# Adding expert rows straight onto the output by accumulating indirect DMAs, in place of a scattered copy that is reloaded and combined

## Chip, cores and metric

One core of a Trainium2 chip runs the whole program. The metric is the device time of one execution in microseconds (us), the median over runs.

## The reference, cut to what matters

A transformer block on 2 sequences of 1024 tokens of width 128, all in float32. The first half (convolution, linear attention, a dense mixture of 4 experts) gives a residual stream `x` after its own scaling by `ga`. The second half, which the change touches, is a routed mixture of 8 experts in which each token uses two of them, and each expert has room for 512 rows:

```python
    h = _layernorm(x, axis=-1) * (1 + cb) + sb
    x = x + gb * _L0_ffn_ref(h, L0_ffn_wg, L0_ffn_w_gate, L0_ffn_w_down)
    # inside _L0_ffn_ref, tokens = h as 2048 rows, C = 512:
    h = jax.nn.gelu(jnp.einsum('ecd,edf->ecf', disp, w_gate), approximate=False)
    eo = jnp.einsum('ecf,efd->ecd', h, w_down).reshape(Ee * C, Dd)
    out = (g1 * keep1)[:, None].astype(x.dtype) * eo[f1] + (g2 * keep2)[:, None].astype(x.dtype) * eo[f2]
```

So each token's output row is its residual row plus `gb` (one row of 128 numbers for each of the two sequences) times the sum of at most two weighted expert rows. An expert slot that holds no token gives nothing.

## The kernel before

Tokens are 16 tiles of 128 rows, worked in 4 blocks of 4 tiles (BT = 4). The first half runs as a software pipeline of 23 steps whose order is written out by hand on each engine, with a semaphore for every hand-over. There is no scheduler: each engine and each queue runs its list in order, and a wait holds all that stands behind it.

The residual after the first half (`x_sb`, "x3" in the names of the semaphores) is made block by block, for blocks 0 to 2 on GpSimd (POOL, lines 387 to 391) and for the last on VectorE (DVE, lines 934 to 940). After that each token's normalised row is written with its number and its two weights (rows of 131 numbers) into the DRAM tensors `line1` and `line2`, a place per expert, by 32 indirect DMAs on POOL's queue (`scatters`, L417). SyncE (SP) waits for the counts (L311), appends the second choices to the first ones (`append`, L307), and loads each expert's 512 rows into SBUF (`rows(e)`, L323, `phi<-line` in the trace).

Then come the 8 experts of 512 rows each, e = 0 to 7. For each:

- TensorE (PE) transposes the rows (L1465), makes the up products (three passes over split operands, in four PSUM banks) and the down products of the expert before. The order on PE is: transposes of e+2, up of e+1, down of e (lines 1485 to 1492); up and down of the last expert close it (lines 1493 to 1497).
- ScalarE (ACT) copies the transposed rows with rounding (L708) and runs four GELUs of 128x512 (L270).
- DVE works out row numbers (`row_addresses`, L1069 to L1076), the low part of the split (L1158), and evacuates the four down products of 128x128, scaled by the row's weight, into the staging buffers `xh` (even experts) or `xm` (odd ones) (L1177).
- POOL issues four indirect DMAs of 128 rows, one per tile (L460), that write the rows into the DRAM tensor `chosen`: 2048 rows for first choices, 2048 for second choices, and behind these a place for empty slots. Rows of `chosen` that no expert writes must be zero, so SP zeroes its first 4096 rows early on (L299).

The last stage waits until all 32 of these DMAs have landed (L328), reloads both halves of `chosen` by 8 DMAs of 256 KB (L331), adds them on POOL (L466), multiplies by `gb` (`modb[..., 3, :]`, L1183) and adds the residual (L1185) on DVE, and stores the output by four DMAs of 256 KB (L334), block by block:

```python
            for half in chosen_written:
                sp.wait_ge(half, 16 * BT * E2 // 2)
            for b in range(NBLK):
                for k in range(2):
                    sp.dma_start(tiles(back[:, k], b), tiles(cv[:, k], b)).then_inc(back_in[b], 16)
            for b in range(NBLK):
                sp.wait_ge(comb_ready, b + 1)
                sp.dma_start(tiles(ov, b), tiles(x_sb, b)).then_inc(stored, 16)
```

DVE's evacuation of expert e from e = 2 on waits until the DMAs of expert e-2 have landed, since the staging buffer is the same.

Of the kernel before, what the change touches and what calls it, by code (L numbers as in the profile page):

```python
# [63 lines left out]
N_CONST = C_TRASH + E2 * BT  # L64


def block_kernel(nc, x, small, proj, wmod, w1, w2, b2, w_up, w_down, const, cmask, out):
    with ExitStack() as ctx:
# [8 lines left out]

        chosen = nc.dram_tensor("chosen", (2 * TOKENS + SLOTS, D), F32).ap()

# [83 lines left out]
        trash = sb("trash", [P, E2, BT])  # L163
        addr = sb("addr", [P, 4, BT])
        row_w = sb("row_w", [P, E2, BT])
        back_i = sb("back_i", [P, E2, BT], U32)

        back = wide[:, 0:TILES * 2 * D].rearrange("p (k t d) -> p k t d", t=TILES, k=2)
# [41 lines left out]
        chosen_written = [sem(f"chosen_written_{i}") for i in range(2)]  # L210
        back_in = L("back_in")
        both_ready, comb_ready, stored = sem("both_ready"), sem("comb_ready"), sem("stored")
# [46 lines left out]
        def xstage(e):  # L259
            return (xh if e % 2 == 0 else xm)[:]  # L260
# [15 lines left out]
        def _(sp):  # L276
            xv = x.rearrange("b (t p) d -> p (b t) d", p=P)
            ov = out.rearrange("b (t p) d -> p (b t) d", p=P)
# [18 lines left out]
            cz = chosen[0:2 * TOKENS, :].rearrange("(p r) d -> p (r d)", p=P)  # L297
            for i in range(BT):
                sp.dma_start(cz[:, i * 1024:(i + 1) * 1024], zero).then_inc(zeroed, 16)  # L299
# [6 lines left out]
            def append(e):  # L306
                sp.dma_start(line1[bass.ds(first[e] + e * LINE1, CAP), :],  # L307
                             line2[e * LINE2:e * LINE2 + CAP, :]).then_inc(moved[e], 16)

# [16 lines left out]
            cv = chosen[0:2 * TOKENS, :].rearrange("(k t p) d -> p k t d", k=2, p=P)  # L326
            for half in chosen_written:
                sp.wait_ge(half, 16 * BT * E2 // 2)  # L328
            for b in range(NBLK):
                for k in range(2):  # L330
                    sp.dma_start(tiles(back[:, k], b), tiles(cv[:, k], b)).then_inc(back_in[b], 16)  # L331
            for b in range(NBLK):
                sp.wait_ge(comb_ready, b + 1)
                sp.dma_start(tiles(ov, b), tiles(x_sb, b)).then_inc(stored, 16)  # L334
            sp.wait_ge(stored, 16 * NBLK)
# [3 lines left out]
        def _(pool):  # L339
# [115 lines left out]
            for e in range(E1):  # L455
                split(2 * E1 + e)
            for e in range(E2):
                for j in range(BT):
                    pool.wait_ge(eout_ready, BT * e + j + 1)
                    g.indirect_dma_start(out=chosen, out_offset=bass.IndirectOffsetOnAxis(back_i[:, e, j:j + 1], 0),  # L460
                                         in_=xstage(e)[:, j, :], in_offset=None).then_inc(chosen_written[e % 2], 16)

            for blk in range(NBLK):
                pool.wait_ge(back_in[blk], 32)
                a, b_ = tiles(back[:, 0], blk), tiles(back[:, 1], blk)
                g.tensor_tensor(a, a, b_, ALU.add).then_inc(both_ready, 1)  # L466
# [3 lines left out]
        def _(act):  # L470
# [20 lines left out]
            def high_part(k):  # L491

                act.wait_ge(wst_in[k // E1], 16)
                if k == E1:
                    act.wait_ge(zeroed, 16 * (E2 + BT))
# [207 lines left out]

            for e in range(E2):
# [4 lines left out]
                if e >= 1:  # L709
                    gelus(act, e - 1)  # L710
            gelus(act, E2 - 1)

        @block.vector
        def _(dve):
# [219 lines left out]
            def residual3(blk):  # L934
# [4 lines left out]
                step(v.tensor_tensor(tiles(x_sb, blk), acc[:], tiles(x_sb, blk), ALU.add))  # L939
                after()  # L940
# [115 lines left out]
            def slot_kinds():  # L1056
# [4 lines left out]
                step(v.scalar_tensor_tensor(trash[:], second[:], -float(TOKENS),  # L1061
                                            c_sb[:, C_TRASH:].rearrange("p (e t) -> p e t", e=E2), ALU.mult, ALU.add))
                after()
# [486 lines left out]
```

## Time and profile before

| | |
|---|---|
| median of 3 runs | 376.99 us (375.58 to 377.82) |
| profiled execution, span from first to last instruction | 385.2 us |
| own time of the profiled execution outside the span | none is given; the span is its time here |
| busy: PE, DVE, POOL, ACT | 72%, 60%, 42%, 38% of the span |
| the 8 experts, from the first transposed rows to the last evacuation | 299.8 to 363.7 us |
| from the last landing in `chosen` to the end | 368.2 to 385.2 us |
| TensorE's granted clock, mean over the span | 0.877 |

The profile is of one execution, on one core, with the profiler on; it is 8.2 us longer than the median of the runs shown. Times in the rows are us from the span's start. A row of the timeline gives start, duration, engine, line, operation, output and inputs, and in brackets the idle time of the engine before it and what ended that. The chain is the work that ended last, followed back step by step.

### The profile page before, as it was taken

The page shows a single profiled execution, that of the slowest core. Times are in us where ns is not written, and L with a number is a line of the kernel's source. Part 1 is how long each engine was busy: PE and PEld are TensorE (multiplying, and loading weights), DVE is VectorE, ACT ScalarE, POOL GpSimd, SP SyncE. Part 2 cuts the span into 40 slices and gives each one's busy share as a digit, 9 for nine tenths or more (in the row PEclk, how much of TensorE's full clock was granted, in tenths as well). Part 3 has the DMA queues.
Part 4 walks back from the last instruction along what each step waited for, and adds up shares of the span by engine and source line. Part 5 has one row for each costly group of instructions (what it writes and reads, how often), then busy time and mean ns, then how long its engine had stood idle before and what let it go on. Part 6 is the DMA issues. An engine that isn't in the chain of part 4 may idle for free.

```text
span 385.2 us, 4892 instructions
## 1 busy us (share of the span) xinstructions
PE 276.5 (72%) x1586; PEld 216.5 (56%) x1586; DVE 230.0 (60%) x678; ACT 148.2 (38%) x278; POOL 161.6 (42%) x165
## 2 busy tenths in 40 slices
PE   2736677656999998988999879994303799999300
PEld 2313333343867687576887768883202589998300
DVE  2478999969578876787498516757550332432116
ACT  3750452358443654326435634450110454451000
POOL 3235585292722126315022532152748116466533
PEclk9995969978699999999999989998555599999955
DMA  7993003000300000000000010000113634211165
GB/s 225 411 375 124 1 1 111 0 1 0 111 1 2 0 2 1 0 3 0 2 0 3 21 37 0 3 29 28 35 37 105 181 101 124 64 41 43 41 195 145
DMA packets 18312, 25.01 MB, mean 65 GB/s; under 512 B 2032, under 2 KB 14448, under 8 KB 17520
## 3 DMA queue, kind: packets, MB, share of 16 engines
q1 hardware_dynamic: 16240, 20.46, 16.4%
q0 software_dynamic: 2048, 4.25, 3.3%
q8 instruction: 13, 0.21, 0.2%
q14 instruction: 11, 0.09, 0.1%
HBM read 15.16 MB, written 11.68 MB: 70 GB/s over the span
## 4 chain that ended last, share of the span: by engine, by line
PE 30%; DVE 12%; issue 6%; DMA 4%; POOL 3%; another core or an unknown queue 3%; ACT 2%; SPq 1%; ACTq 0%; POOLq 0%; DVEq 0%
PE ps L1201 28%; POOL line L417 2%; DVE acc L929 2%; DMA wide<-chosen 1%; DMA phi<-line 1%; PE ps L1465 1%; DVE x_sb L1185 1%; DVE wide L1183 1%; PE ps L1222 1%; DVE nd L852 1%; DMA line<-h3r,dest_i 1%; DVE st L736 1%; ACT hid L600 1%; DVE qp L840 1%
## 5 line engine op out<-in xcount | busy, mean ns | idle before, releaser
L1201 PE MATMUL ps<-w_sb,hid 128*128 128x128 f32 x512 | 63.3, 283 | 5.2 <-DVE acc L929 3.4
L1201 PEld LDWEIGHTS ps<-w_sb,hid 128*128 128x128 f32 x512 | 61.4, 199 | 7.3 <-DVE acc L929 4.0
L600 ACT ACTIVATE hid<-ps,s_sb 128x512 f32<-128x512 f32 x64 | 43.0, 685 | 32.7 <-PE ps L1201 24.9
L414 POOL TENSOR_TENSOR kv<-phi,vx 128x1152 f32<-128x1152 f32 x16 | 38.0, 2375 | 35.0 <-DVE phi L831 15.7
L1201 PE MATMUL ps<-kv,c_sb 128*128 128x512 f32 (+1 forms) x96 | 41.2, 541 | 3.9 <-DVE qp L840 2.0
L417 POOL DMA_INDIRECT line<-h3r,dest_i x32 | 31.4, 980 | 23.3 <-DVE dest_i L1047 14.6
L1201 PE MATMUL ps<-h2h,w1h 128*128 128x512 f32 x80 | 37.1, 463 | 0.5 <-ACT hid L600 0.3
L1201 PE MATMUL ps<-h2l,w1h 128*128 128x512 f32 x80 | 32.5, 407 | 0.0
L1201 PE MATMUL ps<-h2h,w1l 128*128 128x512 f32 x80 | 32.5, 406 | 0.0
L840 DVE TENSOR_TENSOR qp<-ps,phi 128x1024 f32<-128x1024 f32 x16 | 19.5, 1221 | 21.3 <-PE ps L1201 11.6
L1201 PE MATMUL ps<-wd_sb,hid 128*128 128x128 f32 x256 | 30.2, 276 | 1.2 <-issue 1.2
L1201 PEld LDWEIGHTS ps<-wd_sb,hid 128*128 128x128 f32 x256 | 29.8, 192 | 2.2 <-issue 1.6
L929 DVE SCALAR_TENSOR_TENSOR acc<-ps,gwp,acc 128x128 f32<-128x128 f32 x64 | 18.0, 344 | 16.8 <-remote 8.9
L1201 PEld LDWEIGHTS ps<-kv,c_sb 128*128 128x128 f32 x96 | 18.0, 208 | 16.5 <-issue 13.7
L361 POOL TENSOR_SCALAR ve<-mv 128x4 f32<-128x4 f32 x12 | 3.3, 273 | 55.4 <-DVE mv L739 55.3
L460 POOL DMA_INDIRECT chosen<-xh,back_i x16 | 15.4, 961 | 23.7 <-DVE xh L1177 19.7
L270 ACT ACTIVATE hid<-ps 128x512 f32<-128x512 f32 x32 | 19.2, 599 | 12.3 <-PE ps L1201 9.8
L852 DVE TENSOR_REDUCE nd<-qp 128x144 f32<-128x1152 f32 x16 | 21.5, 1345 | 0.1
L460 POOL DMA_INDIRECT chosen<-xm,back_i x16 | 15.3, 959 | 12.3 <-DVE xm L1177 9.0
L708 ACT ACTIVATE h2h<-ps 128x512 fp32r<-128x512 f32 x8 | 4.8, 598 | 39.5 <-PE ps L1465 39.5
L1201 PEld LDWEIGHTS ps<-h2h,w1h 128*128 128x128 f32 x80 | 15.6, 195 | 5.6 <-issue 3.3
L1201 PEld LDWEIGHTS ps<-h2h,w1l 128*128 128x128 f32 x80 | 15.6, 195 | 3.8
(199 smaller groups left out, 535.8 us busy)
## 6 DMA issues: line engine op xcount, KB each, us to landing
line<-wuh SPq DMA_DIRECT2D x8, 262.0 KB, 13.2
line<-line SPq DMA_DIRECT2D x8, 262.0 KB, 3.0
phi<-line SPq DMA_DIRECT2D x8, 262.0 KB, 3.2
wd_sb<-in_w_down SPq DMA_DIRECT2D x1, 2048.0 KB, 12.3
chosen<-wuh SPq DMA_DIRECT2D x4, 512.0 KB, 11.5
wst<-in_w_up SPq DMA_DIRECT2D x2, 1024.0 KB, 5.0
wide<-chosen SPq DMA_DIRECT2D x8, 256.0 KB, 4.9
x_sb<-in_x SPq DMA_DIRECT2D x4, 256.0 KB, 7.3
```

The source lines that it names most:

```text
L270: nc.scalar.activation(hid[:, e % 2, c, :], ps[:, 2 + c, :], ACT.Gelu).then_inc(ehid_ready, 1)
L414: g.tensor_tensor(o_, k_, v_, ALU.mult).then_inc(kv_ready, 1)
L417: g.indirect_dma_start(out=(line1, line2)[k], out_offset=bass.IndirectOffsetOnAxis(dest_i[:, t, k:k + 1], 0), in_=h3r[:, t, :], in_offset= ...
L460: g.indirect_dma_start(out=chosen, out_offset=bass.IndirectOffsetOnAxis(back_i[:, e, j:j + 1], 0), in_=xstage(e)[:, j, :], in_offset=None) ...
L600: a_.activation(hid[:, e % 2, u % FC, :], ps[:, B_UP[u % 2], :], ACT.Silu, bias=s_sb[:, c:c + 1]).then_inc(hid_ready, 1)
L708: a_.activation(h2h[:, e % 2, :], ps[:, e % 2, :], ACT.Copy).then_inc(rowsT_hi, 1)
L736: step(v.bn_stats(st[:, j, :], src[:, j, :]))
L840: v.tensor_tensor(qp[:, 0:DH * D].rearrange("p (m c) -> p m c", m=DH), ps[:, B_KV:B_KV + 2, :].rearrange("p b (m c) -> p (b m) c", m=4), q ...
L852: a = step(v.tensor_reduce(nd[:, 0, :], qp[:].rearrange("p (c d) -> p c d", d=DH), AX.X, ALU.add))
L929: last = v.scalar_tensor_tensor(acc[:, j, :], ps[:, mix_bank(e), j * D:(j + 1) * D], gwp[:, e // E1 % 2, c:c + 1], acc[:, j, :], ALU.mult, ...
L1183: step(v.tensor_tensor(a, a, modb[:, blk // BPB, 3, None, :].broadcast_to([P, BT, D]), ALU.mult))
L1201: return m.matmul(o, l, r, start=start, stop=stop)
```

## The change

The output tensor gets 512 spare rows (SPARE) behind its 2048, which take the empty slots. SP stores the residual `x_sb` into the output as soon as each block of it is there, and zeroes the spare rows. The 8x4 indirect DMAs of POOL now go to the output and add to it (`compute_op=ALU.add`). The factor `gb` must therefore be in the rows before: `gate_rows` makes, for each tile of each expert, the row of `gb` that belongs to the token's sequence, from the masks `half` (token number at most 1024, or above), by an ACT product (`gsel`) and a DVE multiply-add, and the evacuation multiplies by it. Two experts may add to the same row, so POOL waits before the first DMA of expert e until those of expert e-1 have landed (semaphores `added`), and before the first of all until the residual is stored. `chosen`, its zeroing, its reload, the sum, the product, the residual add and the stores at the end are gone.

```diff
 C_ID, C_TRI, C_BD, C_COS, C_SIN, C_REV, C_TOK, C_SLOT, C_TRASH = 0, 128, 256, 400, 464, 528, 536, 552, 556
-N_CONST = C_TRASH + E2 * BT
+N_CONST = C_TRASH + BT
+SPARE = BT * P
...
-        chosen = nc.dram_tensor("chosen", (2 * TOKENS + SLOTS, D), F32).ap()
...
         second = sb("second", [P, E2, BT])
-        trash = sb("trash", [P, E2, BT])
         addr = sb("addr", [P, 4, BT])
+        half = sb("half", [P, E2, 2, BT])
+        gsel = wide[:, 0:2 * BT * D].rearrange("p (a t d) -> p a t d", a=2, t=BT)
         row_w = sb("row_w", [P, E2, BT])
...
-        back = wide[:, 0:TILES * 2 * D].rearrange("p (k t d) -> p k t d", t=TILES, k=2)
...
             xv = x.rearrange("b (t p) d -> p (b t) d", p=P)
-            ov = out.rearrange("b (t p) d -> p (b t) d", p=P)
+            ov = out[0:TOKENS, :].rearrange("(t p) d -> p t d", p=P)
             sp.dma_start(tiles(x_sb, 0), tiles(xv, 0)).then_inc(x_in[0], 16)
...
                              zero[:, 0:BT * ROW]).then_inc(zeroed, 16)
-            cz = chosen[0:2 * TOKENS, :].rearrange("(p r) d -> p (r d)", p=P)
-            for i in range(BT):
-                sp.dma_start(cz[:, i * 1024:(i + 1) * 1024], zero).then_inc(zeroed, 16)
+            sp.dma_start(out[TOKENS:TOKENS + SPARE, :].rearrange("(p r) d -> p (r d)", p=P),
+                         zero[:, 0:BT * D]).then_inc(zeroed, 16)
...
+            for b in range(LAST):
+                sp.wait_ge(x3_ready, b + 1)
+                sp.dma_start(tiles(ov, b), tiles(x_sb, b)).then_inc(x3_stored[b], 16)
+            sp.wait_ge(last_x3, 1)
+            sp.dma_start(tiles(ov, LAST), tiles(x_sb, LAST)).then_inc(x3_stored[LAST], 16)
...
-            cv = chosen[0:2 * TOKENS, :].rearrange("(k t p) d -> p k t d", k=2, p=P)
-            for half in chosen_written:
-                sp.wait_ge(half, 16 * BT * E2 // 2)
-            for b in range(NBLK):
-                for k in range(2):
-                    sp.dma_start(tiles(back[:, k], b), tiles(cv[:, k], b)).then_inc(back_in[b], 16)
-            for b in range(NBLK):
-                sp.wait_ge(comb_ready, b + 1)
-                sp.dma_start(tiles(ov, b), tiles(x_sb, b)).then_inc(stored, 16)
-            sp.wait_ge(stored, 16 * NBLK)
+            for par in range(2):
+                sp.wait_ge(added[par], 16 * BT * E2 // 2)
...
                 split(2 * E1 + e)
+            for blk in range(NBLK):
+                pool.wait_ge(x3_stored[blk], 16)
             for e in range(E2):
+                if e >= 1:
+                    pool.wait_ge(added[(e - 1) % 2], 16 * BT * ((e - 1) // 2 + 1))
                 for j in range(BT):
                     pool.wait_ge(eout_ready, BT * e + j + 1)
-                    g.indirect_dma_start(out=chosen, out_offset=bass.IndirectOffsetOnAxis(back_i[:, e, j:j + 1], 0),
-                                         in_=xstage(e)[:, j, :], in_offset=None).then_inc(chosen_written[e % 2], 16)
-            for blk in range(NBLK):
-                pool.wait_ge(back_in[blk], 32)
-                a, b_ = tiles(back[:, 0], blk), tiles(back[:, 1], blk)
-                g.tensor_tensor(a, a, b_, ALU.add).then_inc(both_ready, 1)
+                    g.indirect_dma_start(out=out, out_offset=bass.IndirectOffsetOnAxis(back_i[:, e, j:j + 1], 0),
+                                         in_=xstage(e)[:, j, :], in_offset=None, compute_op=ALU.add) \
+                        .then_inc(added[e % 2], 16)
...
                 if k == E1:
-                    act.wait_ge(zeroed, 16 * (E2 + BT))
+                    act.wait_ge(zeroed, 16 * (E2 + 1))
                 if k == 2 * E1:
...
+            def gate_rows(e):
+                act.wait_ge(halves_ready, e + 1)
+                if e >= 2:
+                    act.wait_ge(eout_ready, BT * (e - 1))
+                for j in range(BT):
+                    a_.activation(gsel[:, e % 2, j, :], modb[:, 0, 3, :], ACT.Copy,
+                                  scale=half[:, e, 0, j:j + 1]).then_inc(gsel_part, 1)
...
                     gelus(act, e - 1)
+                gate_rows(e)
             gelus(act, E2 - 1)
...
                 after()
-                step(v.tensor_tensor(tiles(x_sb, blk), acc[:], tiles(x_sb, blk), ALU.add))
-                after()
+                v.tensor_tensor(tiles(x_sb, blk), acc[:], tiles(x_sb, blk), ALU.add).then_inc(last_x3, 1)
+                dve.wait_ge(last_x3, 1)
...
                 after()
-                step(v.scalar_tensor_tensor(trash[:], second[:], -float(TOKENS),
-                                            c_sb[:, C_TRASH:].rearrange("p (e t) -> p e t", e=E2), ALU.mult, ALU.add))
-                after()
...
                 number, w_first, w_diff = (rows(e)[:, :, D + i] for i in range(3))
-                step(v.scalar_tensor_tensor(addr[:, 0, :], second[:, e, :], float(TOKENS), number, ALU.mult, ALU.add))
-                step(v.scalar_tensor_tensor(addr[:, 1, :], number, 0.0, trash[:, e, :], ALU.is_equal, ALU.mult))
+                step(v.scalar_tensor_tensor(addr[:, 1, :], number, 0.0, c_sb[:, C_TRASH:C_TRASH + BT],
+                                            ALU.is_equal, ALU.mult))
+                step(v.tensor_scalar(half[:, e, 0, :], number, float(SEQ), None, ALU.is_le))
                 step(v.tensor_tensor(addr[:, 2, :], second[:, e, :], w_diff, ALU.mult))
-                after()
-                step(v.scalar_tensor_tensor(addr[:, 3, :], addr[:, 0, :], -1.0, addr[:, 1, :], ALU.add, ALU.add))
+                v.tensor_scalar(half[:, e, 1, :], number, float(SEQ), None, ALU.is_gt).then_inc(halves_ready, 1)
+                after()
+                step(v.scalar_tensor_tensor(addr[:, 3, :], number, -1.0, addr[:, 1, :], ALU.add, ALU.add))
                 step(v.tensor_tensor(row_w[:, e, :], addr[:, 2, :], w_first, ALU.add))
...
                 dve.wait_ge(back_i_ready, e + 1)
+                dve.wait_ge(halves_ready, e + 1)
+            def gate_rows(e):
+                for j in range(BT):
+                    dve.wait_ge(gsel_part, BT * e + j + 1)
+                    v.scalar_tensor_tensor(gsel[:, e % 2, j, :], modb[:, 1, 3, :], half[:, e, 1, j:j + 1],
+                                           gsel[:, e % 2, j, :], ALU.mult, ALU.add).then_inc(gsel_ready, 1)
...
                     low_part(e + 2)
+                gate_rows(e)
                 if e < E2 - 1:
...
                 if e >= 2:
-                    dve.wait_ge(chosen_written[e % 2], 16 * BT * (e // 2))
+                    dve.wait_ge(added[e % 2], 16 * BT * (e // 2))
                 for j in range(BT):
...
                         dve.wait_ge(edown_ps, e + 1 + j)
-                    v.tensor_scalar(xstage(e)[:, j, :], ps[:, bank, j * D:(j + 1) * D], row_w[:, e, j:j + 1],
-                                    None, ALU.mult).then_inc(eout_ready, 1)
-            for blk in range(NBLK):
-                a = tiles(back[:, 0], blk)
-                dve.wait_ge(both_ready, blk + 1)
-                step(v.tensor_tensor(a, a, modb[:, blk // BPB, 3, None, :].broadcast_to([P, BT, D]), ALU.mult))
-                after()
-                v.tensor_tensor(tiles(x_sb, blk), tiles(x_sb, blk), a, ALU.add).then_inc(comb_ready, 1)
+                    dve.wait_ge(gsel_ready, BT * e + j + 1)
+                    v.scalar_tensor_tensor(xstage(e)[:, j, :], ps[:, bank, j * D:(j + 1) * D], row_w[:, e, j:j + 1],
+                                           gsel[:, e % 2, j, :], ALU.mult, ALU.mult).then_inc(eout_ready, 1)
...
     const[:, C_SLOT:C_SLOT + BT] = np.arange(BT) * P + i[:, None]
-    const[:, C_TRASH:] = 2 * TOKENS + 1 + np.arange(E2 * BT) * P + i[:, None]
+    const[:, C_TRASH:] = TOKENS + 1 + np.arange(BT) * P + i[:, None]
     cmask = np.stack([i[:, None] < i, np.ones((P, P), bool)], axis=1).astype(ml_dtypes.bfloat16)
...
             for k, v in arrays.items()]
-    args.append(nc.dram_tensor("out", (BATCH, SEQ, D), F32, kind="ExternalOutput").ap())
+    args.append(nc.dram_tensor("out", (TOKENS + SPARE, D), F32, kind="ExternalOutput").ap())
     block_kernel(nc, *args)
     r = run_bass_kernel_spmd(nc, [arrays], core_ids=[0])
-    return r.results[0]["out"]
+    return r.results[0]["out"][0:TOKENS].reshape(BATCH, SEQ, D)
```

How the lists of the engines change, as they are issued. POOL's queue from the last weight split on; `eout_ready` counts evacuated tiles, `added_0` and `added_1` the landings of even and odd experts. Before:

```order
L377 TENSOR_TENSOR w1l<-wst,w1h 128x512 [waits w_high] x4
L460 DMA chosen<-xh,back_i 8192x128 [waits eout_ready] x4
L460 DMA chosen<-xm,back_i 8192x128 [waits eout_ready] x4
L460 DMA chosen<-xh,back_i 8192x128 [waits eout_ready] x4
L460 DMA chosen<-xm,back_i 8192x128 [waits eout_ready] x4
```

With the change:

```order
L372 TENSOR_TENSOR w1l<-wst,w1h 128x512 [waits w_high] x4
L459 DMA out<-xh,back_i 2560x128 [waits x3_stored_3,x3_stored_2,eout_ready,x3_stored_1,x3_stored_0]
L459 DMA out<-xh,back_i 2560x128 [waits eout_ready] x3
L459 DMA out<-xm,back_i 2560x128 [waits eout_ready,added_0]
L459 DMA out<-xm,back_i 2560x128 [waits eout_ready] x3
L459 DMA out<-xh,back_i 2560x128 [waits eout_ready,added_1]
L459 DMA out<-xh,back_i 2560x128 [waits eout_ready] x3
```

Each group of four has got a wait for the landing of the group before it, and POOL's four sums of the last stage are gone. The pattern goes on to expert 7.

ACT, from the first transposed rows of expert 0 on (`h2h` is the rounded copy, `hid` a GELU, `wide` holds `gsel`). Before:

```order
L708 ACTIVATE h2h<-ps 128x512 x2
L270 ACT_TABLE_LOAD
L270 ACTIVATE hid<-ps 128x512 x4
L708 ACTIVATE h2h<-ps 128x512
L270 ACTIVATE hid<-ps 128x512 x4
```

With the change:

```order
L712 ACTIVATE h2h<-ps 128x512
L705 ACTIVATE wide<-modb,half 128x128 x4
L712 ACTIVATE h2h<-ps 128x512
L268 ACT_TABLE_LOAD
L268 ACTIVATE hid<-ps 128x512 x4
L705 ACTIVATE wide<-modb,half 128x128 x4
L712 ACTIVATE h2h<-ps 128x512
L268 ACTIVATE hid<-ps 128x512 x4
```

Four products of 128x128 now stand between the GELUs of expert e-1 and the copy for expert e+1; at the end they stand ahead of the last expert's GELUs.

The end of SP's queue, after the load of the last expert's rows. Before:

```order
L323 DMA phi<-line 128x4x131 [waits back_i_ready,rowsT_ps]
L323 DMA phi<-line 128x4x131 [waits back_i_ready,rowsT_ps,moved_7]
L331 DMA wide<-chosen 128x4x128 [waits chosen_written_1,chosen_written_0]
L331 DMA wide<-chosen 128x4x128 x7
L334 DMA out<-x_sb 128x4x128 [waits comb_ready] x4
L68 UNCONDITIONAL_BRANCH [waits stored]
```

With the change:

```order
L304 DMA line<-line 16x4192
L326 DMA phi<-line 128x4x131 [waits back_i_ready,rowsT_ps]
L326 DMA phi<-line 128x4x131 [waits back_i_ready,rowsT_ps,moved_7]
L69 UNCONDITIONAL_BRANCH [waits added_1,added_0]
```

The reload and the stores are gone from the end, and what is left is the wait for all additions. The stores of the residual have moved ahead of the read of the counts.

## Rows read from the trace of the kernel before

**Rows 1.** The chain of work that ended last, from 365 us to the end: start, us, what.

```profile
365.96 2.23 DMA chosen<-xm,back_i
...
368.25 0.37 SPq L331
...
369.76 5.05 DMA wide<-chosen
...
381.56 0.69 DVE x_sb L1185
```

**Rows 2.** DMAs into the output (L334): issue durations and starts; issue to landing.

```profile
L334 SPq DMA_DIRECT2D out<-x_sb x4: 372/374/378, 374.8 to 382.3; - x4
...
DMA to landing us min/median/max: 2.3/2.3/4.1
```

**Rows 3.** Timeline of POOL, first and last scatters into `chosen` (32 in all).

```profile
315.81 0.98 POOL L460 DMA_INDIRECT chosen<-xh,back_i  x1 [15.62 <-DVE xh L1177]
...
319.63 0.96 POOL L460 DMA_INDIRECT chosen<-xh,back_i  x1 [0.30 <-issue]
322.62 0.96 POOL L460 DMA_INDIRECT chosen<-xm,back_i  x1 [2.03 <-DVE xm L1177]
...
349.84 0.96 POOL L460 DMA_INDIRECT chosen<-xm,back_i  x1 [2.05 <-DVE xm L1177]
...
353.63 0.96 POOL L460 DMA_INDIRECT chosen<-xm,back_i  x1 [0.30 <-DVE xh L1177]
354.90 0.96 POOL L460 DMA_INDIRECT chosen<-xh,back_i  x1 [0.30 <-issue]
...
360.64 0.96 POOL L460 DMA_INDIRECT chosen<-xm,back_i  x1 [0.99 <-DVE xm L1177]
363.43 0.96 POOL L460 DMA_INDIRECT chosen<-xm,back_i  x1 [1.84 <-DVE xm L1177]
```

**Rows 4.** Timeline of DVE: evacuations of experts 1, 5, 6, 7.

```profile
321.99 1.13 DVE L1177 TENSOR_SCALAR xm<-ps,row_w 128x128 f32<-128x128 f32 x4 [4.26 <-PE ps L1201]
...
349.21 1.13 DVE L1177 TENSOR_SCALAR xm<-ps,row_w 128x128 f32<-128x128 f32 x4 [4.25 <-PE ps L1201]
352.79 1.13 DVE L1177 TENSOR_SCALAR xh<-ps,row_w 128x128 f32<-128x128 f32 x4 [2.44 <-PE ps L1201]
360.01 0.35 DVE L1177 TENSOR_SCALAR xm<-ps,row_w 128x128 f32<-128x128 f32 x1 [6.09 <-PE ps L1201]
```

**Rows 5.** Loads of an expert's rows from DRAM (L323), 8 of 262 KB: issue to landing.

```profile
L323 SPq DMA_DIRECT2D phi<-line x8: 368/450/575, 296.9 to 330.7; - x8
...
DMA to landing us min/median/max: 2.8/3.2/4.4
```

**Rows 6.** The chain again: the last scatter into `line1`.

```profile
294.28 2.65 DMA line<-h3r,dest_i
```

**Rows 7.** Timeline of ACT: four scaled 128x128 rows; copy and GELUs of a period; the last expert's GELUs.

```profile
95.50 1.64 ACT L480 ACTIVATE xh<-x_sb,shift,rstd 128x128 f32<-128x128 f32 x4
...
322.42 0.60 ACT L708 ACTIVATE h2h<-ps 128x512 fp32r<-128x512 f32 x1 [3.41 <-PE ps L1465]
323.12 2.70 ACT L270 ACTIVATE hid<-ps 128x512 f32<-128x512 f32 x4
...
353.49 1.30 ACT L270 ACTIVATE hid<-ps 128x512 f32<-128x512 f32 x2 [7.25 <-PE ps L1201]
```

**Rows 8.** Timeline of DVE: multiply-adds of 128x128 out of PSUM; the last block's residual.

```profile
264.95 2.29 DVE L929 SCALAR_TENSOR_TENSOR acc<-ps,gwp,acc 128x128 f32<-128x128 f32 x8 [2.08 <-remote]
...
267.99 0.69 DVE L939 TENSOR_TENSOR x_sb<-acc,x_sb 128x512 f32<-128x512 f32 x1
```

**Rows 9.** Waits of SP, longest first: us in total, times, longest.

```profile
SPq L311 <- DVE count_i L1054: 184.6, 1, 184.6
```

**Rows 10.** Timeline of SP: issue of the zeroing of `chosen`.

```profile
16.25 6.15 SPq L299 DMA_DIRECT2D chosen<-wuh  x4
```

More of the change, by code:

```diff
@@ L209, in block_kernel @@
                              "back_i_ready"))
-        chosen_written = [sem(f"chosen_written_{i}") for i in range(2)]
-        back_in = L("back_in")
-        both_ready, comb_ready, stored = sem("both_ready"), sem("comb_ready"), sem("stored")
+        halves_ready, gsel_part, gsel_ready = sem("halves_ready"), sem("gsel_part"), sem("gsel_ready")
+        added = [sem(f"added_{i}") for i in range(2)]
+        x3_stored = L("x3_stored")
+        last_x3 = sem("last_x3")
         LAG = BT + 3
```

## The prediction

> **What bounds the kernel now.** I read the chain of work that ended last first, then the timelines of POOL, DVE and ACT over the eight experts, then the DMA issues. The last of the 32 scatters into `chosen` is issued at 365.96 us and seen landed 2.23 us later, at 368.19; behind it stand only the reload, sum, product, residual and store, to the end at 385.2 us [rows 1]: 17.0 us in which PE and ACT do nothing. Before that PE sets the pace. DVE's evacuations start right when PE ends a down product: in the steady part one expert takes 6.81 us (321.99 to 349.21 in four periods [rows 4]). POOL follows with four DMAs, 3.79 us from the first issue to the last (315.81 to 319.63 with a first one slightly long, 349.84 to 353.63), so 1.26 us apart: 0.96 busy and 0.30 between them. Then it sits idle for 2.05 us until the next expert's first evacuation [rows 3].
>
> **What goes.** After the last landing nothing is left but SP's final wait. Today the last store is issued at 382.3 us and takes 2.3 us to land [rows 2], 384.6 us, so 0.6 us lie between the last landing and the end. With the last landing where it is now, the end would be at 368.2 + 0.6 = 368.8 us: **16.4 us** less. The zeroing of `chosen` (6.15 us of SP's queue at 16.25 us [rows 10]) shrinks to one transfer, but SP then has nothing to issue until it loads weights much later, so I put it at nothing; one transfer of 256 KB in place of four of 512 KB cannot cost anything either.
>
> **What is added beside other work.**
> - The stores of the residual move to where SP is idle: it waits 184.6 us for the counts [rows 9]. The last block is ready at 268.0 + 0.7 = 268.7 us [rows 8], and a store lands in 2.3 to 4.1 us [rows 2], by 273 us; POOL asks for it at 315.8 us, the counts are read at 285. Nothing. Should a store be slow, 40 us of cover stand behind it.
> - ACT gets four scaled 128x128 products per expert. The nearest row takes 1.64 us for four [rows 7]. A period has 0.60 + 2.70 us of work on ACT [rows 7], so with 1.64 it is 4.94 of 6.81. But `gate_rows(e)` waits until expert e-2 is evacuated and stands ahead of the copy for e+1. Counted from the start of the evacuation of e-2: evacuated at 1.13, products to 2.77, copy to 3.4, DVE's low part to 4.1, DVE's own four multiply-adds (8 of them out of PSUM take 2.29 us [rows 8], so 1.15) to 5.3, and the next evacuation is due at 6.81. That leaves 1.5 us. At the end the products of expert 7 run from 350.34 to 352.0 us, and its GELUs start at 353.49 [rows 7]: also 1.5 us. I cost them at nothing; without that cover the price is up to 1.64 us at the end, and as much per period.
> - The evacuation becomes a multiply by a number and a row. Eight such operations take 2.29 us [rows 8], so four take 1.15 against 1.13 us now [rows 4]. The address work gains one operation of 128x4 per expert in DVE's idle time. Nothing.
>
> **What is added on the path.** POOL may no longer issue expert e's first DMA before expert e-1's last has landed. Behind this wait stand its own next issues and nothing else; DVE waits only for the landing of e-2, a whole expert earlier. With a landing as now, a group takes 3.79 (three spacings) + 2.23 (last issue to landing [rows 1]) + 0.30 to start again (360.36 evacuated, 360.64 issued [rows 3, 4]) = 6.32 us. That fits into 6.81 by 0.49 us. Only the end does not fit: experts 5, 6 and 7 are issued today at 349.84, 354.90 and 360.64, expert 6 right behind 5. Chained, they start at 349.84, 356.16 and 362.48, the last landing is at 362.48 + 6.02 = 368.5, and the end at 369.1 us. So the serialisation alone costs 0.3 us.
>
> The unknown is what *adding* costs. Call the extra time to landing a, the extra time of each issue b, and c = a + 4b. Below c = 0.49 the end is at 369.1 + 3c. Above it POOL is the bound from the first expert on, and eight groups carry c each: 315.81 + 7 x (6.32 + c) + 6.02 + c + 0.6 = **366.7 + 8c**.
> - a: the engine has to read the old row from DRAM first. Lower end 0 (the read hidden in the landing of a plain scatter; a gain is excluded, since the same bytes are written). The nearest row that shows a read from DRAM is the load of expert rows, pieces of 524 B like the 512 B here: 3.2 us at the median against 2.3 us for a store of the same size [rows 2, 5]. That is 0.9 us. A scatter of rows of 524 B into `line1` took 2.65 us [rows 6], which would make a 0.4 for reasons that have nothing to do with adding. Upper end: the read is a whole trip of its own, 2.2 us. I take **0.9**, the row of the operation that is new.
> - b: lower end 0, since a POOL issue is the same instruction on the same 128 rows. Upper end 0.48, if three entries must be written per row where two are now: half of 0.96 us again. No row shows a scatter with more than one address list, and I take **0**.
>
> With c = 0.9 the end is at 366.7 + 7.2 = 373.9 us, 11.3 us less than the span of 385.2. The profiled execution is 8.2 us longer than the median of the runs; I take the difference over as it is: 376.99 - 11.3 = **365.7 us**. So of the 16.4 us freed about 5 are given back by the chain of POOL.
>
> **The rivals.**
> 1. *Adding costs almost nothing* (c below 0.49). POOL's idle time swallows it, and the end is at 369.1 to 370.6 us: 361 to 362.4 us in the runs. For it: the whole expert is 256 KB, in a stretch in which the DMA engines have little to do. Against it: a read from DRAM shows 0.9 us. Chance 0.15.
> 2. *Issuing takes half as long again* (b = 0.48, with a = 0.9). POOL's software writes the two sources and the target of each row, so an issue is 1.44 us and a group 9.1 us. POOL is then the bound by 2.3 us per expert (its lag reaches DVE and PE through the staging buffers, which changes nothing for POOL), and the chain takes everything back. c = 2.82, end 389.3 us, **381.1 us in the runs: slower**. It decides from 366.7 + 8c = 385.2, c = 2.3, or b = 0.35 at a = 0.9. For it: 0.96 us for 128 rows is 7.5 ns a row, so the time looks like work per row. Against it: nothing in this trace has a third address. Chance 0.13. The Trainium skill bears on this: "DMA: Bandwidth & Descriptors" (SWDGE vs HWDGE vs iDMA) says that GpSimd's software builds one read and one write descriptor per operation, and "Collectives: The Full Stack" ("Stop ④", where the add happens) shows an add as two reads and one write. By these two pages together the sum would be this rival's 381 us, by the row alone it is 365.7 us, and no run before the change can show which.
> 3. *Read, then write, one after the other* (a about 2.2, b = 0). c = 2.2, end 384.3 us, 376.1 us in the runs: no change. A chance of 0.07 for c from 2.1 to 2.5.
> 4. *The products for the gate row push PE.* If ACT's four products take over 3.1 us or stand in the wrong place, PE waits for the GELUs of each expert. 1 us per period is 7 us, end at about 376 if POOL stays behind: 368 us. Against it the two margins of 1.5 us. Chance 0.05.
> 5. *The change does not do what it says*: the rows are added in an order that needs no wait, or the wait is on a count already reached. The lists show a wait on the right half's semaphore for each group of four. Under 0.01, and it would fall under 1.
>
> **How the numbers follow.** The forecast, c from 0.49 to 2.1 at one end or the other of its costs, has the other 0.59. Cases by c: faster is rival 1, 4 and the forecast itself: 0.80. A measurement of this kernel tells about 0.5% from no change, 1.9 us: no change is c from 2.1 to 2.55, 0.07; slower is c above 2.55, rival 2: 0.13. The range goes from c = 0 with 0.3% of spread between runs, 360 us, up to where no more than 2 in 10 is left out: c = 2.0 gives 374.5, 375 us.
>
> **What would show it.** In the profile after, no work of PE, ACT or DVE behind the last accumulating DMA, and an end 0.6 us behind its landing. The POOL row of the accumulating DMAs gives b against 0.96 us; the idle time of POOL ahead of each group of four, ended by the DMA into the output instead of by DVE, gives 2.23 - 0.96 + 0.3 + a. If a + 4b is over 0.5, the groups stand at equal distances of 6.32 + c from the second expert on and DVE's idle time is no longer ended by PE alone; below it, distances are 6.81 as now. PE's stretch from the first transposed rows to the last down product should be the same within 1 us, unless c is over 2. I am wrong if the first issue of expert 0 moves from 315.8 us by over 1 us, if the distance of groups is over 8.3 us, or if PE waits for ACT or DVE in the steady part.

## The result, and the profile after

The change takes **387.97 us** (median of 4 runs, 383.31 to 389.33) against 376.45 us for the kernel before on the same chip (375.58 to 377.82): a ratio of 1.0295, 95% interval 1.0231 to 1.0359. It is slower by 11.5 us, where 11.3 us less was forecast (365.7); the range ended at 375. Ratios leave out executions that were slower as a whole (here the one of 389.33 us), so they can differ slightly from the ratio of two medians. The profiled execution of the change has a span of 385.6 us and a time of 387.96 us.

The timeline of POOL in the profile of the change, the rows that answer to [rows 3] (first and last issues of groups):

```profile
308.99 1.65 POOL L459 DMA_INDIRECT out<-xh,back_i  x1 [14.86 <-DVE xh L1191]
...
314.67 1.54 POOL L459 DMA_INDIRECT out<-xh,back_i  x1 [0.30 <-issue]
318.19 1.54 POOL L459 DMA_INDIRECT out<-xm,back_i  x1 [1.97 <-DMA out<-xh,back_i]
...
345.77 1.54 POOL L459 DMA_INDIRECT out<-xh,back_i  x1 [1.88 <-DMA out<-xm,back_i]
...
372.94 1.54 POOL L459 DMA_INDIRECT out<-xm,back_i  x1 [1.95 <-DMA out<-xh,back_i]
...
378.49 1.54 POOL L459 DMA_INDIRECT out<-xm,back_i  x1 [0.30 <-issue]
```

An accumulating DMA keeps POOL busy for 1.54 us where a plain one kept it for 0.96 [rows 3]: 0.58 us more for each of the 32. The idle time ahead of a group is ended by the landing of the group before, as the added wait says, and no longer by DVE. Groups stand 9.0 to 9.5 us apart (372.94 - 308.99 = 63.95 us for seven), against PE's 6.8.

The chain of the change, which answers to [rows 1] (start, us, what):

```profile
333.26 3.16 DMA out<-xh,back_i
...
369.45 1.54 POOL out L459
370.99 1.72 issue
...
378.49 1.54 POOL out L459
```

An addition is seen landed 3.16 us behind its issue, where a plain scatter took 2.23 [rows 1]. Of the 0.93 us more, 0.58 are the longer issue, so 0.35 us are the longer landing. (3.16 us is the least of the 32; the median is 3.3 us.) From the third expert on the chain consists of POOL's issues and landings alone, to 380.03 us. Then nothing of it is left, yet the span goes to 385.6. Where these 5.6 us go is in the rows of the last line of the program (instructions that end each engine's list: duration in ns, start) and in SP's waits:

```profile
L69 POOLq DRAIN  x1: 12622/12622/12622, 372.7 to 372.7; - x1
...
L69 SPq DRAIN  x1: 7/7/7, 382.1 to 382.1; - x1
```

```profile
SPq L69 <- PEq L69: 3.5, 1, 3.5
```

A drain can begin while its engine still works through earlier instructions. SP is through at 382.1 us, 0.45 us behind the last landing (378.49 + 3.16 = 381.65). But POOL's drain ends only at 372.7 + 12.6 = 385.3 us, 5.3 us behind POOL's last instruction; the closing instructions of all engines stand behind it, at 385.4 to 385.5 us. The profile names PE as what SP waits for; the times single out POOL, and an experiment below moves POOL's last instruction to test it.

DVE's evacuations stand 6.8 us apart, as before, up to that of expert 3 (328.24 us). From expert 4 on they come late, because the staging buffer of two experts earlier is still being written from; the last one:

```profile
363.66 1.12 DVE L1191 SCALAR_TENSOR_TENSOR xm<-ps,row_w,wide 128x128 f32<-128x128 f32 x4 [6.76 <-DMA out<-xm,back_i]
```

PE is hardly held by this: its matmuls of the experts end at 353.2 us, 57.3 us after the first transposes, where the second profile of the kernel before (below) has 56.1. The four products on ACT cost even less than taken: 1.27 us for four, not 1.64 [rows 7].

### The profile page after: what moved, and what is told of

Same layout as the page of the kernel before. It is cut to its first block, busy times and chain, and to the rows that moved or that the text cites. A ratio compares the mean times of both kernels' runs of the same rounds, so it can differ in the third digit from the quotient of the medians.

```text
span 385.6 us, 4966 instructions
## 1 busy us (share of the span) xinstructions
PE 277.0 (72%) x1586; PEld 215.7 (56%) x1586; DVE 229.9 (60%) x709; ACT 154.5 (40%) x310; POOL 174.8 (45%) x161
## 4 chain that ended last, share of the span: by engine, by line
PE 25%; POOL 10%; issue 10%; DVE 7%; DMA 5%; ACT 2%; POOLq 0%; SPq 0%; ACTq 0%
PE ps L1208 23%; POOL out L459 6%; POOL line L412 4%; DMA out<-xh,back_i 2%; DMA out<-xm,back_i 2%; DVE acc L934 1%; DMA phi<-line 1%; ACT hid L595 1%; PE ps L1472 1%; DVE nd L857 1%; DVE st L741 1%; DMA line<-h3r,dest_i 1%; DVE qp L845 1%; PE ps L1229 1%; POOL rstd L360 1%
## 5 line engine op out<-in xcount | busy, mean ns | idle before, releaser
L1208 PE MATMUL ps<-w_sb,hid 128*128 128x128 f32 x512 | 59.9, 276 | 0.7 <-DVE acc L934 0.7
L1208 PEld LDWEIGHTS ps<-w_sb,hid 128*128 128x128 f32 x512 | 58.8, 192 | 1.8 <-DVE acc L934 0.9
L409 POOL TENSOR_TENSOR kv<-phi,vx 128x1152 f32<-128x1152 f32 x16 | 36.0, 2252 | 34.8 <-DVE phi L836 17.2
L1208 PE MATMUL ps<-kv,c_sb 128*128 128x512 f32 (+1 forms) x96 | 42.9, 562 | 4.1 <-DVE qp L845 2.1
L459 POOL DMA_INDIRECT out<-xh,back_i x16 | 24.9, 1554 | 24.7 <-DVE xh L1191 14.9
L459 POOL DMA_INDIRECT out<-xm,back_i x16 | 24.8, 1552 | 11.5 <-DMA out<-xh,back_i 7.8
L705 ACT ACTIVATE wide<-modb,half 128x128 f32<-128x128 f32 x32 | 10.2, 391 | 23.1 <-DVE xm L1191 11.6
L1208 PEld LDWEIGHTS ps<-h2l,w1h 128*128 128x128 f32 x80 | 15.7, 196 | 2.8 <-issue 0.7
```

Source lines behind the costliest of these rows:

```text
L409: g.tensor_tensor(o_, k_, v_, ALU.mult).then_inc(kv_ready, 1)
L459: g.indirect_dma_start(out=out, out_offset=bass.IndirectOffsetOnAxis(back_i[:, e, j:j + 1], 0), in_=xstage(e)[:, j, :], in_offset=None, co ...
L705: a_.activation(gsel[:, e % 2, j, :], modb[:, 0, 3, :], ACT.Copy, scale=half[:, e, 0, j:j + 1]).then_inc(gsel_part, 1)
L1208: return m.matmul(o, l, r, start=start, stop=stop)
```

## The experiments

Each is the kernel before or the change with the edit shown; where several edits are combined, the text says so. Medians of the kernel before beside them, on the same chip, were 377.4 us (13 runs), 377.5 (17 runs) and 376.9 (3 runs).

**The kernel before, profiled again.** No edit.

> The kernel before, unchanged, profiled once more. Theory A (the first profile of before was of an unusually long execution, so that the span was compared with the wrong base): first scatter of the experts at about 309 us, as in the profile of the change (308.99), and a span of about 374 us. Rival (the change shortens the stages ahead of the experts by 6 to 7 us): first scatter at 315 to 316 us again, span 385 us.

The time is 378.36 us, a ratio of 1.0007 (0.9972 to 1.0042) to the same kernel's other runs: the interval shows that a comparison of this size cannot tell less than 0.4% apart. Timeline of POOL, first, sixth group's first scatter, last scatter, and the sums of the last stage:

```profile
308.35 0.98 POOL L460 DMA_INDIRECT chosen<-xh,back_i  x1 [14.23 <-DVE xh L1177]
...
342.38 0.96 POOL L460 DMA_INDIRECT chosen<-xm,back_i  x1 [2.06 <-DVE xm L1177]
...
356.26 0.95 POOL L460 DMA_INDIRECT chosen<-xm,back_i  x1 [0.30 <-issue]
...
367.18 3.45 POOL L466 TENSOR_TENSOR wide<-wide 128x512 f32<-128x512 f32 x2 [0.97 <-DMA wide<-chosen]
```

The span is 376.2 us (about 374 was expected), and the first scatter stands at 308.35 us, not at 315.81 [rows 3]: the execution profiled first was 9 us longer than this one. Its stages ahead of the experts took 7.5 us more, which say nothing of the change (its own first issue is at 308.99). It also hid something: there expert 7's first tile came 44.2 us after the first scatter (360.01 [rows 4] less 315.81) and its second 47.0 us after it. In this execution DVE evacuates it at 349.37 us, 41.0 us after the first scatter, and POOL issues the last twelve scatters without a pause, 342.38 to 357.2 us. So in this execution, and in the others profiled below without a chain, the scatters of experts 6 and 7 find POOL still busy, and do not wait for PE.

**The change with plain writes** (the addition to the residual is left out).

```diff
-    in_=xstage(e)[:, j, :], in_offset=None, compute_op=ALU.add)
+    in_=xstage(e)[:, j, :], in_offset=None)
```

> The change with plain writes in place of accumulating ones (the addition to the residual is left out, all waits stay). Theory A (adding makes each issue 0.58 us and each landing about 0.35 us longer, and that is what costs): POOL issues of 0.96 us, landings after 2.2 us, groups 6.8 us apart, paced by PE; about 368 us if the end follows POOL's last instruction by 5.4 us (its final drain), about 364 us if it follows the last landing by 0.6 us. Rival B (waiting for the landing of the expert before is what costs, adding is cheap): groups stay about 9 us apart and the time at 387 us.

368.26 us, ratio 0.974 (0.9687 to 0.9794).

```profile
309.24 1.07 POOL L459 DMA_INDIRECT out<-xh,back_i  x1 [14.79 <-DVE xh L1191]
...
343.72 1.13 POOL L459 DMA_INDIRECT out<-xm,back_i  x1 [2.54 <-DMA out<-xh,back_i]
...
350.23 0.96 POOL L459 DMA_INDIRECT out<-xh,back_i  x1 [1.54 <-DMA out<-xm,back_i]
...
360.29 0.96 POOL L459 DMA_INDIRECT out<-xm,back_i  x1 [0.31 <-issue]
```

Issues are 0.96 us again, and chained groups 6.3 us apart (343.72 to 350.23 with a slightly long one). Adding alone is worth 387.97 - 368.26 = **19.7 us** on top of everything else in the change (20.6 us if each is compared with the runs of the kernel before beside it, 19.0 us from POOL's first issue to the end of the profiles). The time also met the figure with the drain (368), not the one without (364): the span ends at 366.8 us, 5.5 us behind POOL's last issue (361.25).

**The kernel before with accumulating scatters**, into the zeroed tensor, no wait added.

```diff
-    in_=xstage(e)[:, j, :], in_offset=None).then_inc(chosen_written[e % 2], 16)
+    in_=xstage(e)[:, j, :], in_offset=None, compute_op=ALU.add).then_inc(chosen_written[e % 2], 16)
```

> The kernel before with its 32 scatters into the zeroed tensor chosen made accumulating, no wait added. Theory A: issues of 1.54 us, 1.85 us apart, four of them 7.4 us, over PE's 6.8: POOL becomes the bound, last landing some 8 us later, 384 us. Rival B: no change, 376 to 377 us.

387.43 us, ratio 1.0251 (1.0181 to 1.0321).

```profile
306.86 1.63 POOL L460 DMA_INDIRECT chosen<-xh,back_i  x1 [14.94 <-DVE xh L1177]
...
314.37 1.54 POOL L460 DMA_INDIRECT chosen<-xm,back_i  x1 [0.31 <-DVE xm L1177]
...
364.27 1.54 POOL L460 DMA_INDIRECT chosen<-xm,back_i  x1 [0.31 <-issue]
```

All 32 issues stand back to back, 7.4 us per expert. Even with no wait at all, the adding makes POOL the bound: 10.1 us. The idle 2.05 us per expert [rows 3] is not quite enough for 4 x 0.58 = 2.3 us, and ahead of experts 6 and 7 there was none. The time is 3 us above the 384 expected: 31 spacings of 1.85 us are 57.4 us, where the second profile of before has 47.9.

**The kernel before with the chain of waits**, plain scatters.

```diff
             for e in range(E2):
+                if e >= 1:
+                    pool.wait_ge(chosen_written[(e - 1) % 2], 16 * BT * ((e - 1) // 2 + 1))
```

> The kernel before with one wait more: POOL issues no scatter of an expert until those of the expert before have landed. Theory A: a group takes 6.3 us, PE's period is 6.8, so only the last two experts are pushed, by 0.3 to 1 us: 376.5 to 377.5 us. Rival B: eight groups of about 9 us, 385 us or more.

381.84 us, ratio 1.0126 (1.0071 to 1.0181): 4.5 us, more than theory A allowed, far less than rival B.

```profile
333.96 1.04 POOL L462 DMA_INDIRECT chosen<-xh,back_i  x1 [2.06 <-DVE xh L1179]
...
341.46 0.95 POOL L462 DMA_INDIRECT chosen<-xm,back_i  x1 [2.69 <-DMA chosen<-xh,back_i]
...
347.74 0.96 POOL L462 DMA_INDIRECT chosen<-xh,back_i  x1 [1.53 <-DMA chosen<-xm,back_i]
...
354.02 0.96 POOL L462 DMA_INDIRECT chosen<-xm,back_i  x1 [1.53 <-DMA chosen<-xh,back_i]
...
357.80 0.96 POOL L462 DMA_INDIRECT chosen<-xm,back_i  x1 [0.30 <-issue]
```

Up to expert 4 PE's period hides the chain, as worked out. The last two groups are 6.28 us apart where they stood 5.05 apart (the second profile of before), and one landing in the middle was late (2.69 us of idle time). From the first scatter to the last issue it is 51.5 us against 47.9; 0.5 us of this is a late evacuation by DVE at the second expert and not the chain. The execution profiled was the shortest of the four (378.77 us; the longest took 383.11), so where the rest of the 4.5 us lies is not shown.

**Both**: kernel before, accumulating scatters and the chain (two edits, the two diffs above together).

> The kernel before with accumulating scatters into the zeroed tensor chosen, and with the wait for the landings of the expert before: the POOL queue of the change with the last stage of before. If the chain and the adding are all that the change costs, groups stand 9.1 us apart, the last landing comes at 381 to 382 us and the end 17 to 18 us behind it: 400 to 402 us. If something else of the change (the stored residual, the gate rows) slows POOL, groups are closer than 9 us and the time is under 398 us.

397.8 us, ratio 1.058 (1.0403 to 1.0757). That is 0.2 us under the line that divides the two forecasts, so the absolute time decides nothing: this execution's first scatter is at 306.31 us and not at 309. The distance from there on decides:

```profile
306.31 1.63 POOL L462 DMA_INDIRECT chosen<-xh,back_i  x1 [12.94 <-DVE xh L1179]
...
375.94 1.54 POOL L462 DMA_INDIRECT chosen<-xm,back_i  x1 [0.30 <-issue]
```

The last issue is 69.6 us behind the first, as in the change (69.5). So the waits and the adding make up the whole lateness of POOL's queue; the stored residual and the gate rows have no part in it.

**Fewer rows per accumulating DMA** (the rest of the expert rows is left out).

```diff
-    IndirectOffsetOnAxis(back_i[:, e, j:j + 1], 0), in_=xstage(e)[:, j, :]
+    IndirectOffsetOnAxis(back_i[0:64, e, j:j + 1], 0), in_=xstage(e)[0:64, j, :]
```

> The change with each accumulating DMA on 64 rows in place of 128 (the other half of the expert rows is left out). Theory A1 (the issue is work per row): issues of 0.8 to 1.0 us in place of 1.54, groups paced by PE at 6.8 us, 366 to 369 us. Rival (the cost of an accumulating DMA is per instruction): issues stay at 1.5 us, groups 9 us apart, 387 us.

383.31 us, ratio 1.0183 (1.0108 to 1.0258), with issues of 1.41 us and groups 8.5 us apart: the theory that the issue is work per row falls. With 32 rows:

> Accumulating DMAs of 32 rows (three quarters of the expert rows are left out). 128 rows took 1.54 us, 64 rows 1.41. If that slope of 2 ns a row holds, 1.34 us; if 64 rows was a floor, 1.41 us again; if an accumulating issue is work per row after all, under 1 us.

And 64 rows written plainly:

> As the run with accumulating DMAs of 64 rows, but plain writes of 64 rows (half of the rows and the addition to the residual are left out). If a plain issue is mostly per instruction too, 0.85 to 0.95 us in place of 0.96; if it is work per row (7.5 ns a row), 0.5 us.

One run each gave 379.21 us (32 rows) and 366.32 us (64 rows, plain). The issues of the even experts in each (ns: minimum, median, maximum), first adding with 64 rows:

```profile
L459 POOL DMA_INDIRECT out<-xh,back_i x16: 1404/1409/1561, 308.6 to 365.1; - x16
```

Adding with 32 rows:

```profile
L459 POOL DMA_INDIRECT out<-xh,back_i x16: 1309/1311/1427, 309.4 to 362.3; - x16
```

Plain with 64 rows:

```profile
L459 POOL DMA_INDIRECT out<-xh,back_i x16: 893/897/965, 307.5 to 352.0; - x16
```

Adding: 1.54 us for 128 rows, 1.41 for 64, 1.31 for 32. Plain: 0.96 for 128, 0.90 for 64. A row costs 2.1 ns (between 64 and 128 rows) with adding and 0.95 ns without. Of the 0.58 us that adding costs per DMA, 128 x 1.15 ns = 0.15 us lie in the rows, and 0.43 us in the instruction itself (an extrapolation along these lines; from 64 to 32 rows the adding form falls by 3.1 ns per row, which would leave about 0.4).

**One POOL instruction more at the end of the change**, after all additions have landed.

```diff
+            for par in range(2):
+                pool.wait_ge(added[par], 16 * BT * E2 // 2)
+            g.memset(mhalf[:], 0.0)
```

> The change with one tiny POOL instruction more, after all additions have landed. Theory D (the end of the program is 5.35 us behind POOL's last instruction, whatever that is): that instruction ends about 1.7 us after POOL's last issue did, so the end moves by 1.7 us, 389.7 us. Rival (the end is 3.7 us behind the last landing): no change, 388 us.

390.93 us, ratio 1.0395 (1.0334 to 1.0455). Timeline of POOL at its end, and the row of its drain:

```profile
378.36 1.54 POOL L459 DMA_INDIRECT out<-xm,back_i  x1 [0.30 <-issue]
381.88 0.10 POOL L464 MEMSET mhalf<- 128x4 f32 x1 [1.98 <-DMA out<-xm,back_i]
```

```profile
L69 POOLq DRAIN  x1: 5417/5417/5417, 381.9 to 381.9; - x1
```

The last issue is where it was (378.36 against 378.49), and the last landing too, but the drain now ends at 387.3 us, 5.35 us behind the memset, and the span grows from 385.6 to 387.5 us. The median is 3.0 us above that of the change, 2.0 if each is compared with the kernel before beside it, where 1.7 was forecast. The end hangs on POOL's last instruction and not on the landing. Why the drain takes 5.3 us is not shown.

**A version that beats both.** The kernel before with the change's gate rows, so that the last stage needs no product, and with POOL out of that stage: two additions per block on DVE. These are several edits; the diff shows those of the last stage, and the gate rows are as in the change.

```diff
-                g.tensor_tensor(a, a, b_, ALU.add).then_inc(both_ready, 1)
...
-                step(v.tensor_tensor(a, a, modb[:, blk // BPB, 3, None, :].broadcast_to([P, BT, D]), ALU.mult))
-                after()
-                v.tensor_tensor(tiles(x_sb, blk), tiles(x_sb, blk), a, ALU.add).then_inc(comb_ready, 1)
+                dve.wait_ge(back_in[0][blk], 16)
+                step(v.tensor_tensor(tiles(x_sb, blk), tiles(x_sb, blk), tiles(back[:, 0], blk), ALU.add))
+                after()
+                dve.wait_ge(back_in[1][blk], 16)
+                v.tensor_tensor(tiles(x_sb, blk), tiles(x_sb, blk), tiles(back[:, 1], blk), ALU.add).then_inc(comb_ready, 1)
```

> The kernel before with the factor gb already in the expert rows (the gate rows of the change), still scattered into chosen; the last stage is two additions per block on DVE alone, POOL does nothing in it. Theory A (the gate rows are hidden; of the last stage's 17.7 us POOL's sums and DVE's product are worth 2 to 4): PE's period stays 6.8 us and the time is 373 to 375.5 us. Rival C (the four ACT products in front of the GELUs push PE): a period over 7 us, the gain gone, 377 us or more.

373.68 us, ratio 0.9896 (0.9862 to 0.993): 1.0% less, a small gain but clear of the spread. Timeline of DVE, two evacuations in the steady part:

```profile
321.02 1.12 DVE L1198 SCALAR_TENSOR_TENSOR xh<-ps,row_w,wide 128x128 f32<-128x128 f32 x4 [1.88 <-PE ps L1223]
327.82 1.13 DVE L1198 SCALAR_TENSOR_TENSOR xm<-ps,row_w,wide 128x128 f32<-128x128 f32 x4 [1.89 <-PE ps L1223]
```

The period is still 6.8 us, with 1.9 us of DVE's idle time left ahead of each evacuation, ended by PE. The gate rows are hidden, and rival C falls. The last stage takes 13.6 us from the last landing (356.11 + 2.23 = 358.3) to the end of the span at 371.9, against 17.7 (358.5 to 376.2). Of these 4.1 us, 0.9 are POOL's drain: in the second profile of the kernel before it ended at 375.9 us, when SP had been through since 375.0; here it is over long before the end.

With four of the eight reloads on ACT's queue:

> As the one before, with half of the eight reloads issued on ACT's queue instead of SP's. If the issue of the reloads (5.5 us on SP) is what the last stage waits for, 1 to 2 us less than that kernel; if it is the transfer of 2 MB, the same within 0.5 us.

373.05 us, ratio 0.9895 (0.9835 to 0.9955), and 13.5 us from the last landing to the end, against 13.6. In its chain one reload stands where SP's issues stood:

```profile
358.63 7.83 DMA wide<-chosen
```

The median is 0.6 us lower, just outside the "same within 0.5", but the intervals overlap and the stage is 0.1 us shorter. So the issue of the reloads on SP was not what the stage waits for; what is left in the chain is their transfer.

## Why the prediction was wrong, point by point

The accounts are made from the first scatter on, since the time ahead of it differs by up to 3.0 us between the executions in this table (306.3 to 309.2 us), and by 7.5 in the first profile.

| profiled execution | first issue to last | last issue to landing | landing to end | sum |
|---|---|---|---|---|
| before, second profile | 47.9 | 2.2 | 17.7 | 67.9 |
| before + chain | 51.5 | 2.2 | 17.0 | 70.7 |
| before + adding | 57.4 | 3.3 | 17.4 | 78.1 |
| before + chain + adding | 69.6 | 3.3 | 16.9 | 89.8 |
| change, plain writes | 51.1 | 2.2 | 4.3 | 57.6 |
| change | 69.5 | 3.2 | 4.0 | 76.6 |

- **What goes** was right in the main: reload, sum, product and stores are gone. Without adding, the time is 9.1 us under before, but not the 15 or so of rival 1: from first issue to end it is 57.6 us, where the prediction's sums give 53.3 for c = 0, and 3.7 of these 4.3 us lie in the end (see below).
- **The extra time of an issue, b, taken as 0, was 0.58 us.** This is the step that failed: the cost of an issue, put at nothing. Alone it turns the sign: with everything else as predicted, b = 0.58 gives c = 3.22, an end at 392.5 and 384.3 us in the runs, slower than before. The text had the right place and a rival with 0.48 us, and gave it a chance of 0.13 because no row of before shows such a DMA. Even its upper end was too low. The reason given for 0 ("the same instruction on the same 128 rows") was wrong: the instruction is another one in cost, and hardly because of its rows.
- **The extra time to landing, a, taken as 0.9, was 0.35 us.** The row of a DRAM load was the wrong neighbour. Together c = a + 4b was 2.67, not 0.9, and 8 x 1.77 = 14.2 us of the error are this.
- **"0.6 us lie between the last landing and the end"** was a coincidence of the kernel before. POOL's drain set its end already: in the profile that the prediction read it ended at 385.0 us, only 0.2 us behind SP's last wait, since POOL's last sum was over 5.3 us earlier:

```profile
L68 POOLq DRAIN  x1: 6663/6663/6663, 378.3 to 378.3; - x1
...
L68 SPq DRAIN  x1: 7/7/7, 384.8 to 384.8; - x1
```

  The change makes a DMA issue POOL's last instruction, and the landing is over long before the drain: the end is 5.6 us behind POOL's last issue and 3.95 us behind the last landing, 3.35 us of the error.
- **The chain alone at 0.3 us** was taken from an execution in which expert 7 came late from PE. In the run with the chain alone it is 3.6 us from first to last issue (0.5 of them DVE's), and 4.5 us in the median. In the change it is part of the formula 366.7 + 8c, so it moved the rival with small c, not the forecast.
- **The base.** From first scatter to end the first profile has 69.4 us, the second 67.9: 1.5 us. Landings above 3.16 us (one group's by 0.56 us) and a few longer issues in the change make the seven groups 1.0 us longer than 7 x 8.99. The four terms 14.2, 3.35, 1.5 and 1.0 give 20.05 us. By the table the change is 76.6 - 67.9 = 8.7 us longer where 11.3 less were forecast, an error of 20.0. By the medians the error is 11.5 + 11.3 = 22.8 us. Of the other 2.8 us, 0.6 are the later first issue, 0.4 the time outside the span (387.96 - 385.6 = 2.4 us against 378.18 - 376.2 = 2.0), and 1.7 that the second profile of before, with 378.18 us, lay above the median 376.45.
- **Adding and chain together cost more than the sum of each.** Alone they are 10.1 and 4.5 us, together 20.9 (397.8 against 376.9), and adding costs 19.7 us where the chain is there already. POOL had 2 us to spare per expert, and either may have it once: the chain uses 1.5 of it unseen, and the 2.3 us of four longer issues, together with the longer landing, then show in full but for the 0.5 us that are left.
- **Rival 2** is what happened, with its direction (slower), its place (POOL's issues) and its form (everything behind the first expert in equal steps of 9.1 us, 9.0 to 9.5 measured). Its mechanism, a third entry per row, can be at most a quarter of the 0.58 us by the runs with fewer rows. The two pages of the Trainium skill that were weighed there ("DMA: Bandwidth & Descriptors" and "Collectives: The Full Stack") pointed to the right side against the row, but what they describe is the descriptors of an operation; neither prices the issue of an indirect DMA, and the runs show 1.31 us for 32 rows, most of which cannot be work per row. What the fixed 0.43 us are, no run here shows.
- **The covers held**: gate rows and evacuations were hidden, as the version that beats both shows by a period of 6.8 us, and the stores of the residual cost nothing that the run with both edits could show. In the change DVE waited for POOL's staging buffers, as rival 2 foresaw. PE did not wait in the steady part; only at the end did it stand 0.5 us for the last expert's GELUs, which came behind ACT's late products.
- **The signs of being wrong.** Groups over 8.3 us apart came true. The first issue moved too, from 315.8 to 309.0 us, but the second profile of before (308.35) shows that this was the base and not the change.

## What to carry to other kernels

A DMA form that the trace does not hold has a price for its issue as well as for its landing, and the issue price is multiplied by the number of DMAs: here 0.58 us x 32 on a queue that had 2 us of slack per expert. When a queue of many small DMAs is near the pace of the bound, measure one such DMA before building on it, and count slack once: a wait and a longer issue cannot both hide in it. The gain was to be had from the last stage itself: moving the product into the expert rows and POOL out of the combine gave 1.0% (0.9896), with plain scatters. What is left untried is adding without the chain: by the table above, 57.4 + 3.3 + 4.0 = 64.7 us from first issue to end, an estimate 3 us under before. No run here shows whether the sums would still be right then, since two experts may add to the same row.

## What the runs showed of the hardware that was not expected

- An accumulating indirect DMA of 128 rows of 512 B holds POOL for 1.54 us, a plain one for 0.96 us. With 64 rows it is 1.41 and 0.90, with 32 rows 1.31: mostly a price per instruction.
- It is seen landed 3.16 us behind its issue at the least (3.3 at the median), against 2.23 us: only 0.35 us more than the longer issue explains.
- POOL's final drain ended 5.3 us (5.27 to 5.35) behind POOL's last instruction in every profile here, the kernel before included, whether that was an indirect DMA (380.03 to 385.3 us in the change), a sum (370.63 to 375.9 in the second profile of before) or a memset (381.98 to 387.3). It costs nothing while other engines work for 5 us longer, as in the version that beats both, where POOL's drain is over at 362.4 us and the span ends at 371.9.
